# Two heads in the two row halves of the array: attention scores and maxima as pairs of 64-row tiles

## The chip, the cores and the metric

One core of a Trainium2 chip. The metric is the device time of one execution in microseconds (us); the time of a kernel is the median of its runs. Engines are named as in the profile: PE is TensorE's matmul part, PEld its weight loads, DVE VectorE, ACT ScalarE, POOL GpSimd, SP SyncE (here it only issues DMAs).

## The reference, cut to what matters

Two attention layers run one after the other on 8 batches of 256 rows of 320 channels, 20 heads of 16 channels each, with 256 context rows. The names in the kernel follow it: a *unit* `u` is one layer of one batch (0 to 7 are layer 0, 8 to 15 layer 1), `q` a running number of a pair of heads.

```python
# layer 0: 77 text tokens and 179 image tokens, one softmax each
q = split_heads(x @ Wq.T); k = split_heads(text @ Wk.T); v = split_heads(text @ Wv.T)
out_text = merge(softmax(q @ k.T / 4) @ v)
out_ip = merge(softmax(q @ k_ip.T / 4) @ v_ip)          # k_ip, v_ip from the image tokens
x = (out_text + out_ip) @ Wo.T + bo + x
# layer 1: 252 text tokens, 4 image tokens; the text weights also form
qsem = l2norm(probs_t @ text_ehs)                        # 512 wide, through a Gram matrix here
fused = q @ k_ip.T / 4 + 0.5 * (qsem @ l2norm(ip_ehs).T)
out = (probs_t @ v + (softmax(fused) * mask) @ v_ip) @ W_out + b_out + x
```

## The kernel before

Sixteen units follow one another, each in ten *slots* `j` (one pair of heads a slot), after a unit -1 that only prepares. `plan(u, j)` writes down by hand what a slot holds, and every engine walks the same plan, so each engine's order is fixed and an engine stops at the first wait that isn't met. In a slot of unit `u` the following stand in a row:

- `scores(q+1)`, line 505: two matmuls (one for each 128 of the 256 tokens `ch`) of 512 columns, two heads side by side, contracted over 100 rows: 96 of split queries and keys (`QP`, `KP`, tile rows 0 to 47 for head `a` = 0 and 48 to 95 for head 1, zero where the other head lies) and rows 96 to 99 that subtract each row's maximum.
- `weights(q+1)`, line 876 on ACT: the exponentials, from the two banks of the scores into `P`. In layer 1 `rounded_weights` (line 866) reads the same banks before that.
- `weigh(u, g)` in even slots, lines 537 to 551: four heads in four 32-column tiles of the array, from `P` (and in layer 1 `Y`) into `pPV`; ACT then copies `pPV` into `Vs` (`evacuate`, line 787) and only after that writes the exponentials of the slot.
- `quad(q, 0)` and `quad(q, 1)` in layer 1, line 519: four and three matmuls of 512 columns with the Gram matrix; DVE multiplies the result into `Y` (line 1116), POOL makes the `Y` it needs (line 1352).
- `maximum(u+1, h)`, line 482: for one head of the *next* unit two matmuls of 256 columns over 96 rows, into one bank; DVE reduces it (lines 1098, 1099 in layer 0, 1101 and 1103 in layer 1). The first of a slot stands before `weigh` in layer 0 and between the two `quad` in layer 1, the others among the projections. There are three in slots 0 to 5 and two in slot 6.
- pieces of the projections of unit `u+2` (lines 388, 415), then `values_back` (`nt`, line 560), and parts of the closing of unit `u-1` (`ot`, `op`, `soft` and others). `soft` in slot 1 of layer 1 makes DVE write `t` (line 1159) and ACT `ex` (line 896), ahead of the slot 2 work of both.

PE's results go to seven PSUM banks, `pB0` to `pB6`. `take` gives the bank that was given back longest ago and makes PE wait until what stood in it has been read (`freed`); so the order of the plan also sets which engine PE waits for.

In slot 7 `shift_rows(u+1)` turns the maxima (line 493); ACT writes `mhi`, DVE `mlo`, and `rows_out` (line 780) sends them by DMA into rows 96 to 99 of `QP`: in layer 0 two DMAs from ACT's queue and two from SP's, in layer 1 two from SP's. `scores` of the next unit, in slot 9, waits for them (`rows_landed`). In slot 8 SP issues the keys of unit `u+2` (line 764, `KP<-k0d`) behind those rows; the first `maximum` of the next unit's slot 0 waits for them (`pack_landed`). For units 8 and 9 POOL fills rows 96 to 99 with 1e20 first (line 1413).

Of the kernel before, what the change touches and what calls it, by code (L numbers as in the profile page):

```python
# [14 lines left out]
U = 2 * B  # L15
# [7 lines left out]
KROWS = 96  # L23
QROWS = 100
# [15 lines left out]
MAXH = (3, 3, 3, 3, 3, 3, 2, 0, 0, 0)  # L40
MAXF = (3, 3, 3, 3, 2, 2, 2, 2, 0, 0)
# [40 lines left out]
def plan(u, j):  # L82
# [17 lines left out]
    many = MAXF if u < 0 else MAXH  # L100
    heads = [("max", u + 1, h) for h in range(sum(many[:j]), sum(many[:j + 1]))] if u + 1 < U else []
    first, rest = heads[:1], heads[1:]
# [3 lines left out]
    scores = [("scores", q + 1)] if u >= 0 and q + 1 < U * NP else []  # L106
    weigh = [("weigh", *divmod(q // 2 - 1, NG))] if q >= 2 and q % 2 == 0 else []
    weigh += [("weights", q + 1)] if scores else []
    if u >= B:
        out += scores + weigh + [("quad", q, 0)] + first + [("quad", q, 1)]  # L110
    elif (u, j) in LATE_MAX:
        out += scores + weigh
        rest = heads
    else:
        out += scores + first + weigh
    out += pieces[0] + pieces[1] + rest[:1] + pieces[2] + rest[1:]
# [58 lines left out]
def build(nc, xT, cT, cipT, fs, Wq0, Wk0, Wv0, Wki0, Wvi0, Wo0, bo0,  # L175
          Wq1, Wk1, Wv1, Wki1, Wvi1, Wo1, bo1, ident_d, ind_d, hm_d, outT):
    with ExitStack() as ctx:
# [18 lines left out]
        wk = sb("wk", [128, 2, EC, C], F32R)  # L196
        wv = sb("wv", [128, 2, EC, C], F32R)
# [4 lines left out]
        ind = sb("ind", [4, 2, S], F32R)  # L202
# [12 lines left out]
        P = sb("P", [128, PR, 2, 2 * S])  # L215
        Y = sb("Y", [128, PR, 2, 2 * S])
# [5 lines left out]
        G = [flat(wk)[:, 0:896], flat(wk)[:, 896:1792], flat(wv)[:, 0:896]]  # L222
        PH = [[flat(wv)[:, 896 + 512 * i:896 + 512 * i + 512] for i in range(2)], [flat(w)[:, at:at + 512] for w, at in ((wv, 1920), (wk, 1792))]]
# [25 lines left out]
        Y_flat = Y[:, :, :, :].rearrange("p a b c -> p (a b c)")  # L249
# [66 lines left out]
        def ind_ready(u):  # L316
            u = u if u < 2 else B + u % 2 if u >= B else u % 2
            return l_ind[u], 16
# [14 lines left out]
        def tensor_program(_):  # L333
# [343 lines left out]
            for u in range(-1, U):  # L677
# [30 lines left out]
                if u < 0:  # L708
                    scores(0)
# [940 lines left out]
```

## Time and profile before

| | |
|---|---|
| median of 3 runs | 806.78 us (806.47 to 809.67) |
| profiled execution | 808.78 us, its span 806.8 us |
| PE / PEld busy | 762.5 / 616.4 us |
| DVE / ACT / POOL busy | 567.9 / 425.4 / 403.0 us |
| a unit of layer 0, of layer 1 | 37.8 us, 54.8 us |

A busy matmul counts from its start to its modelled end, and matmuls overlap in the array, so starts are read rather than durations: how far one row of the timeline starts after the row ahead of it, over the number of instructions in that. A wait shows in brackets at the row that waited.

### The profile page before, as it was taken

The page shows a single profiled execution, that of the slowest core. Times are in us where ns is not written, and L with a number is a line of the kernel's source. Part 1 is how long each engine was busy: PE and PEld are TensorE (multiplying, and loading weights), DVE is VectorE, ACT ScalarE, POOL GpSimd, SP SyncE. Part 2 cuts the span into 40 slices and gives each one's busy share as a digit, 9 for nine tenths or more (in the row PEclk, how much of TensorE's full clock was granted, in tenths as well). Part 3 has the DMA queues.
Part 4 walks back from the last instruction along what each step waited for, and adds up shares of the span by engine and source line. Part 5 has one row for each costly group of instructions (what it writes and reads, how often), then busy time and mean ns, then how long its engine had stood idle before and what let it go on. Part 6 is the DMA issues. An engine that isn't in the chain of part 4 may idle for free.

```text
span 806.8 us, 17013 instructions
## 1 busy us (share of the span) xinstructions
PE 762.5 (95%) x6246; PEld 616.4 (76%) x6246; DVE 567.9 (70%) x1575; ACT 425.4 (53%) x915; POOL 403.0 (50%) x297
## 2 busy tenths in 40 slices
PE   5889999999999999999999999999999999988896
PEld 5777788888788877777877778788777787766574
DVE  5357465757576676858768778698697797686745
ACT  5234646464637373646475565555655655555551
POOL 6511222020202040405568887787779778779763
PEclk9999999999999999999999999999999999999999
DMA  9854735654537372735252354153162332400010
GB/s 282 257 165 145 190 111 154 201 169 138 164 113 200 113 202 75 205 94 158 94 146 91 96 144 152 46 157 115 49 190 70 103 118 66 126 1 17 20 34 17
DMA packets 102514, 100.65 MB, mean 125 GB/s; under 512 B 9752, under 2 KB 101664, under 8 KB 102432
## 3 DMA queue, kind: packets, MB, share of 16 engines
q1 hardware_dynamic: 101952, 99.24, 42.2%
q8 instruction: 50, 0.82, 0.4%
q10 hardware_dynamic: 480, 0.33, 0.2%
q14 instruction: 32, 0.26, 0.1%
HBM read 61.65 MB, written 36.74 MB: 122 GB/s over the span
## 4 chain that ended last, share of the span: by engine, by line
PE 71%; DVE 9%; issue 5%; DMA 5%; ACT 4%; POOL 3%; SPq 2%; POOLq 0%; DVEq 0%; ACTq 0%
PE pB L388 19%; PE pB L519 12%; PE pB L482 8%; PE pB L505 7%; PE pB L603 5%; PE pPV L546 4%; PE pPV L541 4%; PE pPV L551 3%; DMA KP<-k0d 3%; PE pPV L537 2%; PE pB L560 2%; POOL Y L1352 2%; DVE m_sb L1101 2%; PE pB L415 1%; ACT P L876 1%
## 5 line engine op out<-in xcount | busy, mean ns | idle before, releaser
L1352 POOL TENSOR_TENSOR Y<-P,wv 128x512 f32<-128x512 f32 x120 | 157.0, 1326 | 106.6 <-ACT P L876 106.5
L1116 DVE TENSOR_TENSOR Y<-pB,Y 128x512 f32<-128x512 f32 x160 | 109.0, 686 | 67.3 <-PE pB L519 56.8
L482 PE MATMUL pB<-KP,QP 96*128 96x256 f32 x640 | 129.1, 287 | 5.0 <-DMA KP<-k0d 3.6
L1329 POOL TENSOR_TENSOR klo<-xin,khi 128x256 fp32r<-128x256 f32 x18 | 13.2, 756 | 232.1 <-ACT khi L787 232.1
L482 PEld LDWEIGHTS pB<-KP,QP 96*128 96x128 f32 x640 | 106.7, 191 | 17.8 <-issue 5.4
L1101 DVE TENSOR_REDUCE m_sb<-pB 128x2 f32<-128x504 f32 x160 | 108.0, 676 | 6.5 <-PE pB L482 5.3
L505 PE MATMUL pB<-QP,KP 100*128 100x512 f32 x320 | 109.8, 422 | 1.9 <-DMA QP<-mlo 1.5
L876 ACT ACTIVATE P<-pB 128x512 f32<-128x512 f32 x160 | 86.5, 597 | 39.5 <-PE pB L505 29.7
L866 ACT ACTIVATE wv<-pB 128x512 fp32r<-128x512 f32 x120 | 66.8, 591 | 67.3 <-PE pB L505 66.0
L876 ACT ACTIVATE P<-pB,ln 128x512 f32<-128x512 f32 x160 | 101.1, 691 | 0.0
L787 ACT ACTIVATE Vs<-pPV 128x512 f32<-128x512 f32 (+1 forms) x80 | 39.3, 492 | 104.7 <-PE pPV L541 71.3
L1099 DVE TENSOR_REDUCE m_sb<-pB 128x2 f32<-128x358 f32 x160 | 83.2, 520 | 0.0
L388 PE MATMUL pB<-cc,wki 128*128 128x256 f32 (+3 forms) x576 | 80.8, 273 | 0.1
L1098 DVE TENSOR_REDUCE m_sb<-pB 128x2 f32<-128x154 f32 x160 | 49.8, 312 | 41.7 <-PE pB L482 41.0
L519 PE MATMUL pB<-wv,wk 128*128 128x512 f32 x250 | 76.7, 410 | 2.5 <-DVE ipS L1103 2.4
L388 PEld LDWEIGHTS pB<-cc,wki 128*128 128x128 f32 (+1 forms) x576 | 70.6, 172 | 6.5 <-issue 4.1
L388 PE MATMUL pB<-wvi,cc 128*128 128x320 f32 (+1 forms) x384 | 68.0, 314 | 1.0 <-POOL wvi L1342 1.0
L388 PE MATMUL pB<-khi,wq 128*128 128x256 f32 (+1 forms) x288 | 56.7, 292 | 9.9 <-DVE wq L1001 8.5
L388 PEld LDWEIGHTS pB<-wvi,cc 128*128 128x128 f32 x384 | 60.0, 190 | 7.1 <-issue 4.5
L1375 POOL TENSOR_TENSOR rn<-n,mhalf 128x8 f32<-128x8 f32 (+2 forms) x17 | 57.1, 3358 | 15.6 <-DVE n L1147 15.6
L519 PEld LDWEIGHTS pB<-wv,wk 128*128 128x128 f32 x250 | 44.3, 189 | 21.1 <-issue 10.3
L505 PEld LDWEIGHTS pB<-QP,KP 100*128 100x128 f32 x320 | 50.8, 191 | 6.3 <-DMA QP<-mlo 2.3
(175 smaller groups left out, 1477.3 us busy)
## 6 DMA issues: line engine op xcount, KB each, us to landing
QP<-q0d SPq DMA_DIRECT2D x64, 192.0 KB, 4.1
KP<-k0d SPq DMA_DIRECT2D x64, 192.0 KB, 4.2
c_sb<-in_cT SPq DMA_DIRECT2D x16, 512.0 KB, 5.3
q0d<-qhi SPq DMA_DIRECT2D x32, 256.0 KB, 2.4
k0d<-khi SPq DMA_DIRECT2D x32, 256.0 KB, 2.4
q0d<-qlo SPq DMA_DIRECT2D x16, 256.0 KB, 2.5
k0d<-klo SPq DMA_DIRECT2D x16, 256.0 KB, 2.5
VB<-vipd SPq DMA_DIRECT2D x6, 640.0 KB, 3.8
```

Of the source, the lines that this page charges most:

```text
L388: made = mm(out, l, r, start=(n == 0), stop=(n == len(pairs) - 1))
L482: made = mm(bank[:, sc * S:sc * S + S], QP[i][0:KROWS, j, a, sc * 128:sc * 128 + 128], KP[i][0:KROWS, j, :], start=True, stop=True)
L505: mm(bank[:, :], KP[i][0:QROWS, j, ch * 128:ch * 128 + 128], QP[i][0:QROWS, j, :, :].rearrange("p a s -> p (a s)"), start=True, stop=True) ...
L519: made = mm(bank[:, :], G[i][:, col:col + 128], ph[src], start=(n == 0), stop=(n == len(jobs) - 1))
L866: act(PH[q % HR][ch], bank_of["sc", q, ch][:, :], ACT.Exp, scale=0.25).then_inc(ac_ph, 1)
L876: act(P[:, q % PR, ch, :], bank_of["sc", q, ch][:, :], ACT.Exp, scale=0.25, **twice).then_inc(ac_exp, 1)
L1098: nc.vector.tensor_reduce(m_sb[:, :, h], v[:, :, 0:TXT0], AX, ALU.max)
L1099: nc.vector.tensor_reduce(m_sb[:, :, H + h], v[:, :, TXT0:S], AX, ALU.max).then_inc(dv_mx, 1)
L1101: nc.vector.tensor_reduce(m_sb[:, :, h], v[:, :, 0:TXT1], AX, ALU.max)
L1116: tt(Y[:, p, dst, :], bank_of["gp", q, dst][:, :], Y[:, p, dst, :], MUL).then_inc(dv_y, 1)
L1352: tt(Y[:, p, ch, :], P[:, p, ch, :], PH[q % HR][ch].bitcast(F32), SUB).then_inc(po_y, 1)
L1375: tt(rn[:, :, hs], n2[:, :, hs], mhalf[:, 0:2 * n].rearrange("p (c h) -> p c h", c=2), POW).then_inc(po_rn, 1)
```

## The change

Each head gets 64 rows of `QP` and `KP` of its own: head 0 lies in rows 0 to 51, head 1 in rows 64 to 115 (48 of queries and keys, up to 4 that subtract the maximum). `maximum` becomes `maxima(u, j)`: both heads of a pair, four matmuls of 256 columns alternating between the row halves, head 0 into one bank and head 1 into another. `scores` in slots that also hold maxima is done in the same way, four matmuls of 256 columns and 52 rows in place of two of 512 (`halves`); in the other slots it stays two of 512 columns over 116 rows. `PAIRS` sets 2, 1, 2, 0, 2, 1, 2 pairs in slots 0 to 6, and they stand in one block right behind `scores`, ahead of `weigh` and `quad`; in unit -1 and in slot 0 of units 0 and 1 they stand behind most of the projections instead. Each scores bank now holds one head, so ACT writes by head, POOL waits for both heads. `rows_out` sends each row in two DMAs (one for each half), the indicator rows of `KP` go in two as well, and POOL's memset of 1e20 becomes two DMAs on SP's queue for units 8 and 9.

```diff
-MAXH = (3, 3, 3, 3, 3, 3, 2, 0, 0, 0)
-MAXF = (3, 3, 3, 3, 2, 2, 2, 2, 0, 0)
+PAIRS = (2, 1, 2, 0, 2, 1, 2, 0, 0, 0)
+PAIRS_FIRST = (2, 1, 2, 1, 1, 1, 1, 1, 0, 0)
...
+    scores = [("scores", q + 1, halves)] if u >= 0 and q + 1 < U * NP else []
+    out += scores
+    if halves:
+        out += pairs
+    out += [("weigh", *divmod(q // 2 - 1, NG))] if q >= 2 and q % 2 == 0 else []
+    out += [("weights", q + 1, halves)] if scores else []
     if u >= B:
-        out += scores + weigh + [("quad", q, 0)] + first + [("quad", q, 1)]
...
+        out += [("quad", q, 0), ("quad", q, 1)]
+    out += pieces[0] + pieces[1]
+    if late:
+        out += pairs
+    out += pieces[2]
...
+            def maxima(u, j):
+                i = u % 2
+                banks = [take("mx", u * H + 2 * j + a) for a in range(2)]
...
                 for sc in range(2):
+                    for a, bank in enumerate(banks):
+                        rows = half(a, KROWS)
+                        made = mm(bank[:, sc * S:sc * S + S], QP[i][rows, j, a, sc * 128:sc * 128 + 128], KP[i][rows, j, :],
+                                  start=True, stop=True)
...
+                    if halves:
+                        for a, bank in enumerate(banks):
+                            rows = half(a, QROWS)
+                            made = mm(bank[:, ch * S:ch * S + S], KP[i][rows, j, ts], QP[i][rows, j, a, :], start=True, stop=True)
...
             for r, tile, h0 in rows:
...
-                dma(QP[i][r:r + 1, :, :, :].bitcast(F32), tile[h0:h0 + H, :].bitcast(F32)).then_inc(l_m[i], 16)
+                for a in range(2):
+                    row = 64 * a + KROWS + r
+                    dma(QP[i][row:row + 1, :, a, :].bitcast(F32), tile[h0 + a:h0 + H:2, :].bitcast(F32)).then_inc(l_m[i], 16)
...
-                        nc.gpsimd.memset(QP[(u + 1) % 2][KROWS:QROWS, :, :, :].bitcast(F32), 1e20).then_inc(po_big, 1)
...
+                    for a in range(2):
+                        row = 64 * a + KROWS + 2
+                        dma(QP[u % 2][row:row + 1, :, a, :].bitcast(F32),
+                            ind[4:5, 1, None, :].to_broadcast([1, NP, S]).bitcast(F32)).then_inc(l_m[u % 2], 16)
```

Three places show what moves. The names: `KP0,QP0` are the next unit's (a maximum), `QP1,KP1` this unit's (scores), `wv` or `wkv` is a `quad`, `pPV` a `weigh`, `l_ld00` the landing of queries and keys, `ac_exp` the exponentials. First PE in slot 0 of unit 11, before:

```order
L505 MATMUL pB5<-QP1,KP1 128x512 [waits dv_op]
L505 MATMUL pB3<-QP1,KP1 128x512 [waits ac_exp]
L546 MATMUL pPV<-P,VY1 32x256 x8
L551 MATMUL pPV<-Y,y21 32x256 [waits dv_y]
L551 MATMUL pPV<-Y,y21 32x256 x7
L519 MATMUL pB6<-wv 128x512 [waits ac_ph,ac_exp]
L519 MATMUL pB6<-wv 128x512 x3
L482 MATMUL pB2<-KP0,QP0 128x256 [waits l_ld00]
```

and after:

```order
L492 MATMUL pB6<-KP0,QP0 128x256 [waits l_ld00,dv_y,ac_exp]
L492 MATMUL pB2<-KP0,QP0 128x256
L492 MATMUL pB6<-KP0,QP0 128x256
L492 MATMUL pB2<-KP0,QP0 128x256
L492 MATMUL pB3<-KP0,QP0 128x256 [waits dv_op,dv_y]
L492 MATMUL pB4<-KP0,QP0 128x256
L492 MATMUL pB3<-KP0,QP0 128x256
L492 MATMUL pB4<-KP0,QP0 128x256
L569 MATMUL pPV<-P,VY1 32x256 x8
L574 MATMUL pPV<-Y,y21 32x256 x8
```

The first matmul that needs the next unit's keys has moved ahead of `weigh` and of the first `quad`. Next PE in slot 2 of unit 11, from its scores on, before:

```order
L505 MATMUL pB0<-QP1,KP1 128x512 [waits dv_mx]
L505 MATMUL pB5<-QP1,KP1 128x512 [waits dv_y]
L546 MATMUL pPV<-P,VY2 32x256 x8
L551 MATMUL pPV<-Y,y21 32x256 x8
L519 MATMUL pB4<-wv 128x512 [waits ac_ph,dv_bg,ac_bg]
L519 MATMUL pB4<-wv 128x512 x3
```

and after (left out are the eight matmuls of the maxima, into `pB0`, `pB6`, `pB1` and `pB2`):

```order
L522 MATMUL pB4<-QP1,KP1 128x256 [waits dv_mx]
L522 MATMUL pB5<-QP1,KP1 128x256
L522 MATMUL pB4<-QP1,KP1 128x256
L522 MATMUL pB5<-QP1,KP1 128x256
...
L569 MATMUL pPV<-P,VY2 32x256 x8
L574 MATMUL pPV<-Y,y21 32x256 x8
L542 MATMUL pB4<-wkv 128x512 [waits ac_ph,ac_exp]
L542 MATMUL pB4<-wkv 128x512 x3
L542 MATMUL pB5<-wkv 128x512 [waits ac_exp]
L542 MATMUL pB5<-wkv 128x512 x2
```

The first `quad` now goes into `pB4`, the bank of this same slot's scores, where it had another bank. Last SP around slot 7 of unit 4, before:

```order
L735 DMA k1d6<-klo 64x256
L780 DMA QP1<-mlo 1x20x256 [waits dv_sr,ac_sr]
L780 DMA QP1<-mlo 1x20x256
L764 DMA KP0<-k0d6 48x4x256 [waits l_k]
L764 DMA KP0<-k0d6 48x4x256
```

and after:

```order
L758 DMA k1d6<-klo 64x256
L803 DMA QP1<-mlo 1x10x256 [waits dv_sr,ac_sr]
L803 DMA QP1<-mlo 1x10x256 x3
L787 DMA KP0<-k0d6 48x4x256 [waits l_k]
L787 DMA KP0<-k0d6 48x4x256
```

Four DMAs of the row `mlo` stand ahead of the keys where two stood.

## Rows read from the trace of the kernel before

**Rows 1.** The page: busy time of the engines; the chain that ended last.

```profile
PE 762.5 (95%) x6246; PEld 616.4 (76%) x6246; DVE 567.9 (70%) x1575; ACT 425.4 (53%) x915; POOL 403.0 (50%) x297
...
PE 71%; DVE 9%; issue 5%; DMA 5%; ACT 4%; POOL 3%; SPq 2%; POOLq 0%; DVEq 0%; ACTq 0%
```

**Rows 2.** Busy time by stretch: unit 5, unit 10 (columns in the first row).

```profile
core 0: us, PE busy (x) PEld busy (x) DVE busy (x) ACT busy (x) POOL busy (x), PEclk, DMA share, GB/s
246.40:284.20 37.80, 37.66 (x347) 31.71 (x344) 25.81 (x76) 20.91 (x47) 4.24 (x6) 1.00 0.58 165
472.30:527.10 54.80, 53.97 (x431) 43.19 (x429) 44.64 (x117) 31.14 (x66) 43.08 (x30) 1.00 0.38 114
```

**Rows 3.** Timeline of PE, unit 2: start us, us, engine, line, operation.

```profile
150.97 0.40 PE L482 MATMUL pB<-KP,QP 96*128 96x256 f32 x2
151.30 0.64 PE L537 MATMUL pPV<-P,VX 77*32 77x256 f32 x8
...
156.87 0.63 PE L505 MATMUL pB<-QP,KP 100*128 100x512 f32 x2
157.34 0.40 PE L482 MATMUL pB<-KP,QP 96*128 96x256 f32 x2
157.58 0.66 PE L388 MATMUL pB<-cc,wki 128*64 128x180 f32 x6
```

**Rows 4.** Weight loads by line and shape (busy us, mean ns | idle); timeline of eight loads.

```profile
L482 PEld LDWEIGHTS pB<-KP,QP 96*128 96x128 f32 x640 | 106.7, 191 | 17.8 <-issue 5.4 <-DVE m_sb L1099 1.5 <-ACT P L876 0.8
...
L537 PEld LDWEIGHTS pPV<-P,VX 77*32 77x32 f32 x320 | 6.3, 108 | 7.6 <-issue 3.6
...
151.30 0.16 PEld L537 LDWEIGHTS pPV<-P,VX 77*32 77x32 f32 x8
```

**Rows 5.** Timeline of slot 4 of unit 11: PE and ACT around a weighing.

```profile
553.25 1.07 PE L546 MATMUL pPV<-P,VY 128*32 128x256 f32 x16
...
554.13 1.05 PE L551 MATMUL pPV<-Y,y 128*32 128x256 f32 x16
...
555.11 1.20 PE L519 MATMUL pB<-wv 128*128 128x512 f32 x4
555.25 0.38 ACT L787 ACTIVATE Vs<-pPV 128x256 f32<-128x256 f32 x1 [1.04 <-PE pPV L551]
...
555.53 1.26 ACT L876 ACTIVATE P<-pB,ln 128x512 f32<-128x512 f32 x2
```

**Rows 6.** Timeline of slot 2 of unit 11: PE and ACT.

```profile
544.33 1.21 PE L519 MATMUL pB<-wv 128*128 128x512 f32 x4
...
544.88 0.34 ACT L896 ACTIVATE ex<-t 128x160 f32<-128x160 f32 x1 [2.76 <-DVE t L1159]
...
546.34 1.28 ACT L876 ACTIVATE P<-pB,ln 128x512 f32<-128x512 f32 x2
```

**Rows 7.** Timelines of SP's queue and PE from unit 4's slot 7 to unit 5's slot 0.

```profile
242.08 1.64 SPq L780 DMA_DIRECT2D QP<-mlo  x2
243.76 1.25 SPq L764 DMA_DIRECT2D KP<-k0d  x2
...
246.38 0.71 PE L505 MATMUL pB<-QP,KP 100*128 100x512 f32 x2
...
248.58 0.47 PE L482 MATMUL pB<-KP,QP 96*128 96x256 f32 x2
```

**Rows 8.** DMA issues by line: KB each, median us from issue to landing.

```profile
KP<-k0d SPq DMA_DIRECT2D x64, 192.0 KB, 4.2
...
KP<-k1d SPq DMA_DIRECT2D x32, 96.0 KB, 3.1
```

**Rows 9.** Timelines of SP's queue and PE from unit 11's slot 8 into slot 0.

```profile
529.08 1.27 SPq L764 DMA_DIRECT2D KP<-k0d  x2
...
531.03 0.63 PE L505 MATMUL pB<-QP,KP 100*128 100x512 f32 x2
...
533.46 1.19 PE L519 MATMUL pB<-wv 128*128 128x512 f32 x4
534.48 0.40 PE L482 MATMUL pB<-KP,QP 96*128 96x256 f32 x2
```

**Rows 10.** Waits: engine line waited for: us in total, times, longest.

```profile
PE pB L493 <- DVE ipS L1103: 4.3, 8, 1.7
```

More of the change, by code:

```diff
@@ L22 @@
 NP = H // 2
-KROWS = 96
-QROWS = 100
+KROWS = 48
+QROWS = 52
+IROWS = 16
 PR = 3
@@ L99, in plan @@
         pieces = [[], [], []]
-    many = MAXF if u < 0 else MAXH
-    heads = [("max", u + 1, h) for h in range(sum(many[:j]), sum(many[:j + 1]))] if u + 1 < U else []
-    first, rest = heads[:1], heads[1:]
+    many = PAIRS_FIRST if u < 0 else PAIRS
+    pairs = [("max", u + 1, jj) for jj in range(sum(many[:j]), sum(many[:j + 1]))] if u + 1 < U else []
+    late = u < 0 or (u, j) in LATE_MAX
+    halves = bool(pairs) and not late
     out = []
@@ L495, in shift_rows, with scores @@
                 give(bank)
-            def scores(q):
+            def scores(q, halves):
                 u, j = divmod(q, NP)
@@ L502, in scores @@
                 pe.wait_ge(*ind_ready(u))
+                banks = [take("sc", q, n) for n in range(2)]
                 for ch in range(2):
-                    bank = take("sc", q, ch)
-                    mm(bank[:, :], KP[i][0:QROWS, j, ch * 128:ch * 128 + 128],
-                       QP[i][0:QROWS, j, :, :].rearrange("p a s -> p (a s)"), start=True, stop=True).then_inc(pe_sc, 1)
+                    ts = slice(ch * 128, ch * 128 + 128)
+                    if halves:
+                        for a, bank in enumerate(banks):
+                            rows = half(a, QROWS)
+                            made = mm(bank[:, ch * S:ch * S + S], KP[i][rows, j, ts], QP[i][rows, j, a, :], start=True, stop=True)
+                            if ch == 1:
+                                made.then_inc(pe_sc, 1)
+                    else:
+                        rows = slice(0, 64 + QROWS)
+                        mm(banks[ch][:, :], KP[i][rows, j, ts], QP[i][rows, j, :, :].rearrange("p a s -> p (a s)"),
+                           start=True, stop=True).then_inc(pe_sc, 1)
+                for bank in banks:
                     give(bank)
@@ L681, in tensor_program @@
                         if what == "max":
-                            maximum(*a)
+                            maxima(*a)
                         elif what == "bg":
@@ L708, in tensor_program @@
                 if u < 0:
-                    scores(0)
+                    scores(0, False)
             weigh(U - 1, NG - 1)
@@ L1280, in vector_program @@
                         if what == "max":
-                            maximum(*a)
+                            for h in (2 * a[1], 2 * a[1] + 1):
+                                maximum(a[0], h)
                         elif what == "done":
```

144 lines of the change are left out of this document (69 added, 75 removed).

## The prediction

> **What bounds the kernel now.** The page first: PE is busy for 95% of the span and makes up 71% of the chain that ended last [rows 1]. By stretch it is the same everywhere, but its margin is not: in unit 5 (layer 0) PE is busy 37.7 of 37.8 us and DVE 25.8 (68%); in unit 10 (layer 1) PE 54.0 of 54.8, DVE 44.6 (81%) and POOL 43.1 (79%) [rows 2]. So time saved on PE is time saved until one of four late arrivals takes over: a bank that ACT or DVE has not read yet, the rows of maxima, the next unit's keys, or DVE itself. The timelines show how far off each is, and it is very little. I read them at the places to which the change moves a wait.
>
> **What PE saves.** Starts in the timeline: two maximum matmuls take 157.34 to 157.58, 0.12 us each; two of the scores 156.87 to 157.34, 0.235 each [rows 3]. Two heads in two row halves should stream at once, two matmuls of 256 columns in the 0.12 us of one.
> - Maxima: a pair has four matmuls, 0.48 us before, 0.24 after; 160 pairs (10 in each of 16 preparing stretches): -38.4 us.
> - Scores: of 160 slots 88 are done by halves (slots 0, 1, 2, 4, 5, 6 of units 0 to 14, less slot 0 of units 0 and 1): 0.47 before, 0.24 after: -20.2 us.
> - Change of tiling: before the column tiles of a weighing the last maximum pair takes 150.97 to 151.30, 0.33 where 0.24 is usual [rows 3]; after it 554.13 to 555.11 is 0.98, where the sixteen ahead of it took 0.88 [rows 5]. So a change costs 0.09 to 0.10 us. Even slots with a block gain one (full, halves, columns, full), odd ones and the late blocks two: 58 + 60 + 20 = 138 changes: +13.8 us.
>
> Whether the pair really runs at once hangs on the weight loads, which the trace shows for columns only. A load of 128 columns takes 191 ns in the records, one of 32 columns 108 [rows 4]: 0.86 ns a column, so about 110 ns of loading for 128, as long as the 0.12 us of the matmul it hides behind. Side by side in both halves that still fits; one after the other it would take 0.22 us a pair of matmuls and eat the gain. Eight loads of 32 columns for the weighing all stand within 0.16 us, each of them 108 ns [rows 4], so they do overlap between column tiles. I take "at once"; the other is a rival. (The Trainium skill, TensorEngine Tiling (Array Packing), Key Properties, says that different tiles load and multiply in parallel and that a changed tiling mode drains the array; the drain agrees with the 0.09 us of the rows, the parallel load in row halves no row here shows.)
>
> PE alone would thus give -44.8 us. Now what comes late.
>
> **Rows of maxima (slot 7 to 9, layer 0).** Two `mlo` DMAs are issued in 1.64 us, 0.82 each, the last at 242.9; small loads into these tiles land 3.1 us after issue [rows 7, 8], so at 246.0, and the scores that wait for them start at 246.38 [rows 7]. Slots 7 to 9 hold no maxima, so PE gets there as before. The rows go out in four DMAs now: two more at 0.8 each, 1.6 us, less about 0.2 of slack (0.4 by the median): +1.5 for each of units 0 to 7, 12 us. At unit 8 four more stand on SP (two halves, two of 1e20): 3.2 less some slack, +2.7. The POOL memset that goes hid behind other work and gives nothing back. If half a row costs half the issue the term falls from 14.7 to 7.
>
> **Keys.** SP issues the keys right behind these rows in layer 0: the second at 244.4, which lands 4.2 later at 248.6 [rows 7, 8], and the first maximum starts at 248.58 [rows 7]. No slack: they come 1.6 later, PE has lost 1.5 of that already; and in unit 8: +2 in all. In layer 1 they are anchored to the closing of the unit before, not to the rows: issued at 529.1 and 529.7, landing at 533.9; the first maximum starts at 534.48 [rows 8, 9], late, because weighing and the first quad stand ahead of it. In the new order it stands 0.3 behind scores that start at 531.03 [rows 9]: 531.3. PE then waits 2.6 us, and weighing and both quads queue behind it.
>
> **Banks behind the exponentials.** In even slots 2, 4, 6 of layer 1 the first quad now takes a bank of this slot's scores. ACT frees it after `Vs`, which waits for the weighing, and one exponential: `Vs` starts at 555.25, the exponentials at 555.53, the first done at 556.2; the quad starts at 555.11 [rows 5]. So 1.1 us of idle PE where no other bank was needed before. Slots 4 and 6, units 8 to 13: 12 x 1.1 = +13.2. In layer 0 it is the last piece of the projections in slot 4 (seven short matmuls cover part of it) and `nt`: 0.5 a unit, and one late slot 0: +5.
>
> **Slots 0 to 2 of layer 1.** In slot 2 ACT is later still: `ex` waits for DVE's `t`, and only then come the roundings, `Vs` and the exponentials from 546.34, the first done at 547.0, against the quad's start at 544.33 [rows 6]: 2.7. That chain starts with DVE, which has as many maxima and products ahead of `t` as before, and starts its maxima about 1.9 later through the keys: exponential at 548.9. PE without waits would be at 543.8 (544.33, -0.9 for slots 0 and 1, -0.2 for the scores, +0.6 for two pairs and a change). 5.1 us, keys included. The seven units differ in how early their keys are (unit 8 and 9 have slack, 14 waited already): I take 4.2 as a mean, +29.3 us. It is the largest term, and the least sure: 2 to 5 a unit.
>
> **Given back.** The shift in slot 7 waited for the last maximum, 4.3 us over 8 units [rows 10]; the block in slot 6 stands earlier: -4.3.
>
> **Sum**: -38.4 - 20.2 + 13.8 + 14.7 + 2 + 13.2 + 5 + 29.3 - 4.3 = +15.1 us. Against the profiled execution's own 808.8 that is 823.9; the median of the runs is 2.0 lower, 806.8, so I forecast 822 (824 for an execution like the profiled one).
>
> (The Trainium skill, TensorEngine Tiling, PSUM Bottleneck, warns that tiling speeds TensorE but not the reading of PSUM. That is the mechanism of the terms on banks, in this kernel's order; without it the sum would be some 40 us lower.)
>
> **Rivals.**
> 1. *Loads of the two halves go one after the other.* Then a pair of matmuls takes two loads, 0.22 us, and pair and scores gain next to nothing: -4.8 and -1.8 in place of -58.6. Some 12 us of that are hidden in slots 0 to 2 of layer 1, which wait anyway: 822 + 52 - 12 = 862. Against it: the overlapping column loads; for it: no row shows a load in a row half. 0.18.
> 2. *The chain to the exponentials is not late, and half rows cost half.* DVE then keeps up in slots 0 and 1 (it has 19% of the unit idle, and the odd slots lose a maximum), so slots 0 to 2 cost 1.2 each unit, 8 rather than 29, and the rows 7 rather than 15: 822 - 21 - 8 = 793, faster than before. It decides from a mean cost of some 2 us in slots 0 to 2. Against it: keys and `t` are both read as late, by rows. 0.11.
> 3. *Nothing but PE counts*, all waits hidden: 762. 0.03.
> 4. *The forecast*, with its terms off by up to their bounds: 808 to 845. 0.62, of which 0.03 lies within 4 us of before.
> 5. Between 1 and 4, a load that overlaps in part: 845 to 860. 0.06.
>
> **How the numbers follow.** 822, the likeliest. The range leaves out rival 3, a third of rival 2 and most of rival 1: 792 to 852. 0.5% is about what a measurement of this kernel can tell from no change, 802.7 to 810.8. Faster: rivals 3 and 2, 0.13. Same: 0.07, from the edges of 2 and 4. Slower: 0.80.
>
> **What would show it.** Right: maxima in blocks of four starting at 0.12 a pair; PE waits before L542 for the exponentials of about 1.1 us in slots 4 and 6 of units 8 to 13, and more in slot 2; a wait for keys at L492 in slot 0 of layer 1, of 2 to 3 us; a wait for `QP<-mlo` before the scores of slot 9 in each unit of layer 0; units of layer 0 near 37 us and of layer 1 near 58. Wrong: a cadence of 0.22 a pair (rival 1); layer 1 units under 54.8 (rival 2); no wait on `mlo` (the rows' price). If units of layer 0 are slower than 38, the price of pairs or of changes of tiling is off.

## The result, and the profile after

| | before | after |
|---|---|---|
| median of 4 runs, us | 808.22 (806.47 to 809.96) | 870.74 (865.26 to 876.89) |
| profiled execution, us (span) | 808.78 (806.8) | 865.26 (863.5) |
| granted clock, mean of the span | 0.989 | 0.974 (0.959 to 0.964 in the other runs) |

The change makes the kernel 7.7% slower: ratio 1.0771, 95% interval 1.0728 to 1.0814. I had forecast 822 us, range 792 to 852. The sign was right, the size was not: +62.5 us where +15 was worked out.

The page of after has this row where the first of [rows 1] stood. PE's busy time fell by only 8 us, while the span grew by 57:

```profile
PE 754.8 (87%) x6422; PEld 581.0 (67%) x6422; DVE 573.1 (66%) x1575; ACT 424.3 (49%) x915; POOL 394.5 (46%) x295
```

The same two units as in [rows 2], unit 5 and unit 10, with the same columns. Both are longer, and in both PE is busy for less time than before (36.4 for 37.7, 52.7 for 54.0), DVE, ACT and POOL for as long as before:

```profile
249.90:289.50 39.60, 36.37 (x359) 29.08 (x357) 25.76 (x76) 20.62 (x47) 4.23 (x6) 1.00 0.58 157
493.20:553.30 60.10, 52.71 (x442) 40.83 (x441) 45.45 (x117) 31.17 (x66) 43.23 (x30) 1.00 0.36 103
```

**What stops PE now.** Waits of PE in after (line waited for: us in total, times, longest). L492 are the maxima, L542 the quads, L583 the transposes of values:

```profile
PE pB L542 <- ACT P L905: 24.7, 19, 2.5
PE pB L492 <- DMA KP<-k0d: 20.9, 12, 2.8
PE pB L492 <- DVE klo L1030: 9.0, 9, 1.2
...
PE pB L492 <- DVE alo L1030: 7.7, 8, 1.7
PE pB L583 <- ACT Vs L810: 6.1, 9, 2.8
...
PE pB L492 <- DVE qlo L1030: 3.1, 7, 0.7
```

In before the quads never waited for an exponential, the maxima never for a low part, and for keys they waited 3.6 us:

```profile
PE pB L482 <- DMA KP<-k0d: 3.6, 4, 2.5
```

**The balance.** I walked PE's instructions from start to start. The time up to the next start is PE's own, less what the records show as idle; of the time at 1.2 GHz, the lower of the clock's two levels, half counts as lost to the clock. The 8.5 us ahead of PE's first instruction are left out. Over the profiled executions, in us:

| | before | after | difference |
|---|---|---|---|
| PE's own work, at the full clock | 757.0 | 735.5 | -21.5 |
| idle ahead of an instruction | 32.8 | 97.3 | +64.5 |
| lost to the clock (half of 17.1 and 44.4 us at 1.2 GHz) | 8.6 | 22.2 | +13.6 |

That is +56.6, the whole difference between the two profiled executions. The other runs of after had a lower clock still, and the median is some 5 us longer than the profiled one. Three things are to be explained: a gain of 21.5 where I had 44.8, waits of 64.5 where I had 60, but partly in other places, and the clock, for which I had nothing.

**The pairs do run at once.** Timeline of PE, unit 4 of after: one block of two pairs between scores by halves and a weighing.

```profile
229.64 0.50 PE L522 MATMUL pB<-QP,KP 52*128 52x256 f32 x4
229.98 0.64 PE L492 MATMUL pB<-KP,QP 48*128 48x256 f32 x8
230.55 0.64 PE L560 MATMUL pPV<-P,VX 77*32 77x256 f32 x8
```

Eight maximum matmuls take 0.57 us to the next start; one after the other they would take 0.95. In the records the two heads' matmuls here start 4 ns apart and the next two 0.118 us later, so the weight loads of the halves overlap and rival 1 falls. But the four matmuls of the scores take 0.34 us and not 0.24: the first load in a new tiling stands exposed, 0.10 us, and it has no place in my sum.

**The first long wait.** Unit 12, slot 0: the scores at 620.84, then PE stands still until the keys have landed. I had worked out 2.6 us from the rows of unit 11. In units 10 to 14 it is 1.9 to 2.8 (2.81 in unit 11), here 2.14.

```profile
620.84 0.50 PE L522 MATMUL pB<-QP,KP 52*128 52x256 f32 x4
623.48 0.74 PE L492 MATMUL pB<-KP,QP 48*128 48x256 f32 x8 [2.14 <-DMA KP<-k0d]
624.15 1.51 PE L569 MATMUL pPV<-P,VY 128*32 128x256 f32 x16
```

What follows shows in the windows of the same place: for 3.42 us right behind this wait PE has a granted clock of 0.50, that is 1.2 of 2.4 GHz, and the sixteen matmuls of L569, usually 0.88, take 1.26 to the next start.

```profile
616.80:624.63 7.83, 5.69 (x48) 4.47 (x50) 7.38 (x17) 4.82 (x11) 7.83 (x3) 1.00 0.68 147
624.63:628.05 3.42, 3.42 (x30) 1.68 (x23) 2.47 (x8) 0.64 (x2) 0.95 (x1) 0.50 1.11 223
```

**The exponentials.** Unit 11, slot 2, the place of [rows 6]:

```profile
574.48 0.50 PE L492 MATMUL pB<-KP,QP 48*128 48x256 f32 x4 [0.34 <-DVE qlo L1030]
574.91 1.07 PE L569 MATMUL pPV<-P,VY 128*32 128x256 f32 x16
...
576.18 0.34 ACT L925 ACTIVATE ex<-t 128x160 f32<-128x160 f32 x1 [2.41 <-DVE t L1189]
...
577.38 0.39 ACT L810 ACTIVATE Vs<-pPV 128x256 f32<-128x256 f32 x1
...
577.64 1.28 ACT L905 ACTIVATE P<-pB,ln 128x512 f32<-128x512 f32 x2
...
578.40 1.89 PE L542 MATMUL pB<-wkv 128*128 128x512 f32 x7 [1.55 <-ACT P L905]
```

The chain is the one I described: `ex` waits for DVE's `t`, and only behind it come the roundings, `Vs` and the exponential that frees the quad's bank.

### The profile page after: what moved, and what is told of

The parts are those of the page before. It is cut to its first block and busy times, and to the rows that moved or that the text cites. A ratio compares the mean times of both kernels' runs of the same rounds, so it can differ in the third digit from the quotient of the medians.

```text
span 863.5 us, 17573 instructions
## 1 busy us (share of the span) xinstructions
PE 754.8 (87%) x6422; PEld 581.0 (67%) x6422; DVE 573.1 (66%) x1575; ACT 424.3 (49%) x915; POOL 394.5 (46%) x295
## 5 line engine op out<-in xcount | busy, mean ns | idle before, releaser
L1384 POOL TENSOR_TENSOR Y<-P,wkv 128x512 f32<-128x512 f32 x160 | 207.6, 1321 | 158.6 <-ACT P L905 158.1
L542 PE MATMUL pB<-wkv 128*128 128x512 f32 x560 | 152.4, 409 | 25.8 <-ACT P L905 24.7
L542 PEld LDWEIGHTS pB<-wkv 128*128 128x128 f32 x560 | 101.1, 190 | 71.6 <-ACT P L905 36.1
L895 ACT ACTIVATE wkv<-pB 128x512 fp32r<-128x512 f32 x160 | 86.3, 592 | 75.2 <-PE pB L522 36.7
L492 PE MATMUL pB<-KP,QP 48*128 48x256 f32 x640 | 67.1, 299 | 45.6 <-DMA KP<-k0d 20.9
L492 PEld LDWEIGHTS pB<-KP,QP 48*128 48x128 f32 x640 | 48.9, 187 | 56.6 <-issue 45.1
L395 PE MATMUL pB<-cc,wki 128*128 128x256 f32 (+3 forms) x576 | 76.1, 276 | 1.5 <-ACT P L905 1.5
L395 PEld LDWEIGHTS pB<-cc,wki 128*128 128x128 f32 (+1 forms) x576 | 68.3, 172 | 11.4 <-issue 4.5
L395 PEld LDWEIGHTS pB<-khi,wq 128*128 128x128 f32 (+1 forms) x288 | 42.9, 182 | 15.9 <-DVE wq L1030 8.5
L527 PE MATMUL pB<-QP,KP 116*128 116x512 f32 x144 | 50.4, 433 | 2.6 <-DMA QP<-ind 1.6
```

Source lines behind the costliest of these rows:

```text
L395: made = mm(out, l, r, start=(n == 0), stop=(n == len(pairs) - 1))
L492: made = mm(bank[:, sc * S:sc * S + S], QP[i][rows, j, a, sc * 128:sc * 128 + 128], KP[i][rows, j, :], start=True, stop=True)
L527: mm(banks[ch][:, :], KP[i][rows, j, ts], QP[i][rows, j, :, :].rearrange("p a s -> p (a s)"), start=True, stop=True).then_inc(pe_sc, 1)
L542: made = mm(bank[:, :], G[i][:, col:col + 128], ph[:, src, :, :].rearrange("p a s -> p (a s)"), start=(n == 0), stop=(n == len(jobs) - 1))
L895: act(split(PH[q % HR], n, halves), scored(q, n), ACT.Exp, scale=0.25).then_inc(ac_ph, 1)
L1384: tt(y, w, r.bitcast(F32), SUB).then_inc(po_y, 1)
```

## The experiments

Theory A: the place of the blocks is the loss (keys, exponentials and low parts are late there). Theory B: the halves themselves cost (changes of tiling, exposed loads). Theory C: the clock is a loss of its own. Each run is given with the kernel before timed beside it.

### Slot 0 behind the projections

```
-LATE_MAX = ((0, 0), (1, 0))
+LATE_MAX = tuple((u, 0) for u in range(U))
```

> The changed kernel, but in slot 0 of every unit the pairs stand behind the projections (and the scores of that slot go over full rows), as they do in units 0 and 1. Theory A (the place of the blocks costs: keys and banks are late there): the wait for keys before the first maximum (20.9 us in all, nearly all in slot 0) goes, what is left of it is 3 us or less; the scores of 13 slots cost 0.23 more each (+3); part of what slot 0 gives comes back as a later wait in slot 2, since DVE gets the maxima no sooner. 850 to 860 us against 870.7. Theory B (the row halves themselves cost: changes of tiling, exposed weight loads): the time stays within 4 us of 870. Theory C (the clock: waits let it fall and that costs most): as A, and the time at 1.2 GHz (44 us) falls by a third.

854.7 us, ratio 1.0564 (1.0512 to 1.0617), against 1.0771: 16 us less. The wait for keys is gone from the waits of PE; units 2 to 4 of layer 0 take 38.7, 38.6 and 38.7 us where they took 41.3, 38.7 and 38.9. Theory A as written, B's "within 4 us" is out. Theory C is not borne out as written: the time at 1.2 GHz should have fallen by a third and fell from 44 to 41 us. In the units whose wait had gone, 10 to 13, there was none, but units 5 and 9 have stretches where after has none.

### Every block behind the projections

```
+LATE_MAX = tuple((u, j) for u in range(U) for j in range(NP))
```

> The changed kernel with every block of pairs behind the projection pieces of its slot; maxima stay pairs in the two row halves, all scores go over full rows. Theory A: the waits before maxima and before the quads (71 us of the 97 that PE waits) go back to about 10, the time at 1.2 GHz from 44 to about 20; PE's own work is 745 without the clock, + 20 for full scores, - 5 for fewer changes of tiling: 760, with 45 of waits and 8 for the clock 813 us, range 800 to 825: about as before (808). Theory B: the pairs still cost their changes and exposed loads, and the time stays above 840. Rival within A: DVE then gets the maxima of a slot in one late heap and the shift in slot 7 waits for it; units of layer 1 then stay near 58 us.

856.8 us (1.0586; 1.0522 to 1.0649). 813 was wrong. The quads waited 0, as expected, but the shift took the wait over, as in the rival inside A:

```profile
PE pB L505 <- DVE ipS L1132: 17.1, 8, 3.9
PE pB L505 <- DVE m_sb L1128: 12.2, 8, 2.3
```

Maxima at the end of a slot reach DVE in a heap, and in slot 7 the shift stands behind the last of them. Own work was also 2 us a unit above the changed kernel's in layer 0 (38.2 for 36.3): full scores and isolated blocks. The time at 1.2 GHz, expected to fall to about 20 us, was 47.8.

### The order alone

```
-                        rows = half(a, KROWS)
+                        rows = slice(0, 64 + KROWS)
...
-    scores = [("scores", q + 1, halves)] if u >= 0 and q + 1 < U * NP else []
+    scores = [("scores", q + 1, False)] if u >= 0 and q + 1 < U * NP else []
```

> The order of the changed kernel without the halves: maxima and scores of every slot over full rows (112 and 116), one after the other, the blocks where the change puts them. The maxima then take in rows that hold the mask, so the result is not the reference's; every operation of the other engines is the same. Theory A: PE does 58 us more of work, less 19 for changes of tiling and first loads, and much of that is hidden under the same waits: 865 to 885 us, no quicker than the changed kernel, with waits of 50 to 70 us. Theory B: without row halves the time falls below 850.

910.4 us (1.1266; 1.1189 to 1.1343), above the range. The edit brought a wait of its own: the full rows need the rows of `ind`, which I had overlooked.

```profile
PE pB L493 <- DMA KP<-ind: 35.2, 4, 10.3
PE pB L543 <- ACT P L906: 23.2, 20, 2.3
PE pB L493 <- DMA KP<-k0d: 16.7, 9, 2.9
```

So the total says little; the units without that wait do: own work 38.3 us in units 3 to 5 and 54.4 in units 10 to 13, where the changed kernel has 36.3 and 52.4. The halves save 2.0 us a unit against the same order over full rows, 32 us in sixteen units; my 58.6 less 13.8 for changes is 44.8. The waits for exponentials and keys are there without any half: they belong to the order. And this order costs 0.7 and 0.3 us a unit of own work against before, with no half in it. (Its matmuls also go over 112 and 116 rows where before has 96 and 100; no run separates the two.)

### Full scores

```
-    scores = [("scores", q + 1, halves)] if u >= 0 and q + 1 < U * NP else []
+    scores = [("scores", q + 1, False)] if u >= 0 and q + 1 < U * NP else []
```

> The changed kernel with all scores over full rows, blocks of maxima still in halves and still ahead of the weighing. Plain sum: 88 slots by 0.23 us are 20 us more of PE work with the same number of changes of tiling, half of it under waits: 875 to 885. Rival D (scores by halves make the exponentials late: both banks are done only at the end, where over full rows the first is done 0.23 us sooner, and GpSimd waits for both): the time is at or below 870, and the waits of quads for the exponentials (24.7 us) fall by a third or more.

868.6 us (1.0732; 1.0674 to 1.0791), level with the changed kernel. Own work rises by 1.0 us a unit and the waits fall by as much (7.7 to 6.8 in units 10 to 13). The scores by halves, 20 us of my sum, give nothing in this order. The quads' wait did not fall by a third (23.9 for 24.7), so rival D's reason is not shown; the plain sum is wrong as well.

### Blocks of two in the odd slots

```
-PAIRS = (2, 1, 2, 0, 2, 1, 2, 0, 0, 0)
+PAIRS = (1, 2, 1, 2, 1, 2, 1, 0, 0, 0)
```

> The changed kernel with the blocks of two pairs in the odd slots (1, 2, 1, 2, 1, 2, 1 pairs in slots 0 to 6), where no weighing follows. Theory A1 (the quads wait for the exponentials because a block of two pairs, the scores and the weighing come together in an even slot): the 24.7 us of the quads' wait for ACT fall under 8, the wait for keys stays; 840 to 852 us. Theory A2 (the DVE is what is late and hands banks back late wherever the block stands): the waits move to the odd slots, their sum falls by less than 10 us, 858 to 868.

848.2 us (1.0486; 1.0416 to 1.0555). The time is inside A1's range, with a little more left than it said:

```profile
PE pB L492 <- DMA KP<-k0d: 20.4, 12, 2.6
PE pB L542 <- ACT P L905: 9.6, 12, 0.9
```

The wait for keys is there as in the changed kernel (20.4 for 20.9), the quads' fell from 24.7 to 9.6. The waits are those of the profiled execution, which took 858.2 us, 10 more than the median.

### The second pair behind the projections

```
-    if halves:
-        out += pairs
+    if halves:
+        out += pairs[:1]
...
-    if late:
-        out += pairs
+    out += pairs if late else pairs[1:]
```

> The changed kernel, but of a block of two pairs only the first stands ahead of the weighing and the second behind the projection pieces. Theory A1: no slot takes more than six banks before its quads: their wait for the exponentials falls under 5 us; keys stay (20 us); 10 to 12 more changes of tiling than now in each unit (+ 0.5 us each unit); 840 to 850. Theory A2: 858 or more.

838.6 us (1.0338; 1.0294 to 1.0381), the best single move: 32 us, 1.4 more than A1 allowed. The quads' wait is gone, the wait for low parts ahead of maxima fell from 19.8 to 0.9, and the keys' stays (17.9). Some of it came back at the shift (13.3 us, DVE) and before late pairs (7.5, ACT). A1 holds: a slot with two pairs ahead takes 2 + 4 banks, the projection under way holds the last of the seven, and so the first quad gets one that ACT still has to read. With one pair ahead it does not.

### The pairs alone

In layer 0 the first pair of a slot behind the scores, in layer 1 between the quads, a second one behind the projections, 2, 1, 2, 1, 2, 1, 1 pairs, full scores:

```
+    first = [] if late else pairs[:1]
+    if u < B:
+        out += first
...
-        out += [("quad", q, 0), ("quad", q, 1)]
+        out += [("quad", q, 0)] + first + [("quad", q, 1)]
```

> The order of the kernel before as near as pairs allow (2, 1, 2, 1, 2, 1, 1 pairs; the first of a slot behind the scores in layer 0 and between the quads in layer 1, a second one behind the projection pieces), with maxima as pairs in halves and all scores over full rows. PE's own work: 10 pairs save 2.4 us in a unit, 20 changes of tiling (0.09) and 10 exposed first loads (0.10) cost 2.8: as before, 54 in layer 1 and 37.6 in layer 0. Theory A: waits are nearly those of before, 808 to 822 us. Rival (heads that come two at a time are late for DVE and for the banks whatever the order): waits of 2 us and more in each unit, 830 to 850.

825.0 us (1.0175; 1.0138 to 1.0211), 3 us above the range. The window of unit 10: PE is never idle, and yet the unit is no shorter than before (54.9; before 54.8 with 0.8 idle):

```profile
485.90:540.80 54.90, 54.90 (x430) 40.87 (x429) 44.12 (x117) 31.10 (x66) 43.03 (x30) 1.00 0.39 113
```

So ten pairs, which save 2.4 us of matmuls, raise the own work by 0.9 (54.9 for 54.05): their changes and loads cost 3.3 us, 0.33 a block. This is theory B's part. With so few waits there is no time at 1.2 GHz in units 0 to 14 either.

### Half of DVE's maxima

```
-                    nc.vector.tensor_reduce(m_sb[:, :, h], v[:, :, 0:TXT1], AX, ALU.max)
+                    nc.vector.tensor_reduce(m_sb[:, :, h], v[:, :, 0:TXT1 // 2], AX, ALU.max)
```

(and 88 of 179 columns in layer 0)

> The changed kernel with half of DVE's work on the maxima taken away: the maxima of the scores of 88 of 179 and 126 of 252 columns only, so the result is not the reference's; PE, ACT and GpSimd do the same. DVE is busy some 2.5 us less in a unit of layer 0 and 5 in one of layer 1. Theory A2 (DVE is late): the waits for low parts (20 us) and for the exponentials (24.7) fall by half or more, 835 to 850 us. Theory A1 (the place and ACT's own order make them late): they stay, 862 to 870.

864.7 us (1.0676; 1.0629 to 1.0723). The waits did not move:

```profile
PE pB L542 <- ACT P L905: 25.6, 20, 2.8
PE pB L492 <- DMA KP<-k0d: 21.0, 13, 2.8
PE pB L492 <- DVE klo L1030: 9.0, 9, 1.2
...
PE pB L492 <- DVE alo L1030: 8.0, 8, 1.7
```

DVE's load is not the cause, though its name stands in two of the rows. Slot 4 of unit 11 in the trace of after shows what is:

```profile
585.49 0.57 ACT L810 ACTIVATE khi<-pB 128x504 fp32r<-128x504 f32 x1
585.61 0.31 PEld L492 LDWEIGHTS pB<-KP,QP 48*128 48x128 f32 x4
585.72 0.40 PE L492 MATMUL pB<-KP,QP 48*128 48x256 f32 x4
...
586.09 0.47 DVE L1030 TENSOR_TENSOR klo<-kip,khi 128x8 fp32r<-128x8 f32 x1 [1.02 <-ACT khi L810]
586.49 0.67 DVE L1030 TENSOR_TENSOR klo<-pB,khi 128x504 fp32r<-128x504 f32 x1
...
587.30 0.50 PE L492 MATMUL pB<-KP,QP 48*128 48x256 f32 x4 [1.19 <-DVE klo L1030]
```

The second pair of the block wants the bank of the projection that has just ended. DVE, idle for 1.02 us, waits for ACT's copy of it and reads the bank only then.

### Both moves together

Slot 0 behind the projections and second pairs late.

> The changed kernel with both moves that took waits away, together: slot 0 of every unit behind the projections, and in the other slots only the first pair of a block ahead of the weighing. Theory A (waits and the clock that they take along are the loss; own work of PE is then 37.4 us in units 3 to 5 and 53.2 in 10 to 13 where the kernel before has 37.6 and 54.05): the waits fall to some 1 us a unit and the time at 1.2 GHz in units 8 to 14 to 7 us or less; 812 to 824 us, at best level with before, since the pairs have almost nothing to give. Rival (the pairs still have 20 us in them): 800 or less. Rival (the two moves take the same wait): 835.

825.9 us (1.0194; 1.0162 to 1.0227): 45 us less than the changed kernel, where the two moves alone took 16 and 32. They are nearly additive, so they take different waits. The waits did not fall to 1 us a unit but to 1.9 in units 10 to 13, 1.1 of it before maxima and 0.7 at the shift, and the time is 2 us above the range. Units 8 to 14 still have 13.6 us at 1.2 GHz where I had said 7 or less.

### Half rows in the kernel before

```
-                dma(QP[i][r:r + 1, :, :, :].bitcast(F32), tile[h0:h0 + H, :].bitcast(F32)).then_inc(l_m[i], 16)
+                for a in range(2):
+                    dma(QP[i][r:r + 1, :, a, :].bitcast(F32), tile[h0 + a:h0 + H:2, :].bitcast(F32)).then_inc(l_m[i], 16)
```

> The kernel before with one part of the change alone: each row of maxima goes out as two DMAs of half the heads, 8 in place of 4 in each unit of layer 0, 4 in place of 2 in layer 1. The prediction's term: 1.5 us a unit in layer 0, 12 and more in all: 819 to 824 us. Rival (a half row is issued in the same 0.8 us but lands sooner, as the trace of the changed kernel has it: 2.05 us after the last issue): 0.5 us a unit, 810 to 814.

818.1 us against 809.8, ratio 1.0099 (1.0074 to 1.0125): 8 us, 6 to 10. That is between my 14.7 and the rival, but it is not the wait that I had priced. PE waits for `mlo` once, in unit 0, for 1.1 us (1.5 in before), and in no other unit of layer 0. Two other waits grew, from 3.6 us for keys and 4.7 for the transposes' `Vs`:

```profile
PE pB L560 <- ACT Vs L788: 7.1, 10, 2.8
PE pB L482 <- DMA KP<-k0d: 6.9, 7, 3.2
```

Between the two profiled executions the clock took 3.4 us more, too. The later `Vs` has a cause at hand that I had overlooked: ACT's own queue also sends two rows in layer 0, four now, ahead of its exponentials and the next `Vs`. Around slot 7 of unit 4, before and with half rows:

```profile
241.26 1.52 ACTq L780 DMA_DIRECT2D QP<-mhi  x2
```

```profile
246.62 3.05 ACTq L781 DMA_DIRECT2D QP<-mhi  x4
```

No run halves ACT's rows alone, so this stays argued. On SP's side the trace of after shows why the scores of slot 9 need not wait. SP's queue and PE from unit 4 to unit 5, the place of [rows 7]:

```profile
245.28 3.15 SPq L803 DMA_DIRECT2D QP<-mlo  x4
248.47 0.61 SPq L787 DMA_DIRECT2D KP<-k0d  x1
```

```profile
249.52 0.63 PE L583 MATMUL pB<-ident,Vs 128*128 128x128 f32 x4 [0.23 <-ACT Vs L810]
249.91 0.71 PE L527 MATMUL pB<-QP,KP 116*128 116x512 f32 x2
```

Four issues take 3.15 us, 0.79 each, as expected. But by the semaphore's records the last half row lands 2.05 to 2.07 us after its issue begins (six places in layer 0), where the last whole row in before took 3.1 to 3.5. I had taken 3.1 for both. Half rows so delay the rows by some 0.5 us and not by 1.6, and 0.2 of that is behind PE's wait for `Vs`.

### The wait for keys filled

Seven matmuls of 512 columns in units 8 to 14, into the bank that the maxima then overwrite:

```
+                for _ in range(7 if j == 0 and u > B else 0):
+                    mm(banks[0][:, :], wo[:, 0, 0, 0:128], wo[:, 0, 1:3, 0:256], start=True, stop=True)
                 pe.wait_ge(*pack_landed(u, j // 4))
```

> The changed kernel with seven matmuls of 512 columns (1.65 us, results overwritten) put ahead of the wait for keys in slot 0 of units 8 to 14, where PE stands idle for 1.8 us and more. Theory C (the idle time takes the clock down and that is a loss of its own): PE reaches the first maximum when it did, and the stretches at 1.2 GHz that begin some 7 us into units 10 to 14 (3.4 us each, at least five) do not come: 8 to 12 us less than the changed kernel, 858 to 864. Rival (the row halves and small tiles take the clock down, not the idle time): the stretches stay, and the time is that of the changed kernel or some us more.

859.6 us (1.0598; 1.0559 to 1.0637) against 1.0771: 11 us less, with 12 us more of matmuls. The granted clock of its four runs is 0.974 to 0.986, that of after's 0.959 to 0.974. (The two profiled executions, after's fastest and this kernel's slowest, are only 4 us apart; there the clock's share is 6.8 us.) The same slot of unit 12:

```profile
621.26 0.50 PE L524 MATMUL pB<-QP,KP 52*128 52x256 f32 x4
621.69 1.88 PE L488 MATMUL pB<-wo 128*128 128x512 f32 x7
623.95 0.74 PE L494 MATMUL pB<-KP,QP 48*128 48x256 f32 x8 [0.39 <-DMA KP<-k0d]
624.62 1.07 PE L571 MATMUL pPV<-P,VY 128*32 128x256 f32 x16
```

The maxima come 2.69 us behind the scores, as in after (2.64), and the clock stays, in this stretch and in the whole of unit 12:

```profile
625.00:628.40 3.40, 3.40 (x39) 1.99 (x28) 3.19 (x9) 1.54 (x3) 1.16 (x2) 1.00 1.12 217
...
617.20:677.70 60.50, 54.65 (x450) 42.15 (x449) 45.52 (x117) 31.12 (x66) 43.28 (x30) 1.00 0.38 103
```

Theory C is shown for this wait: with the same halves and small tiles in place, the stretches of units 11 to 13 went with the idle time ahead of them, so it was the idle time that took the clock down. It does not do so each time. Of units 8 to 13 only unit 9 has such a stretch left, behind a quad's wait of 2.44 us, and in after the same wait was 2.52 us and no stretch followed. Two others came in units 3 and 5, where nothing was edited and after has none. In units 2 to 14 of after nine waits are 1.9 us or longer, and at six of them the clock fell.

### Pairs alone, halves for the scores of layer 0

```
-    halves = bool(pairs) and not late
+    halves = bool(pairs) and not late and u < B
```

on the kernel of the pairs alone, with the scores by that flag.

> The order of the kernel before with pairs (as in the run of the pairs alone, 825 us), and in layer 0, where the first pair of a slot stands right behind the scores, the scores of these slots by halves too: seven slots of a unit save 0.23 us each and no change of tiling is added, 1.6 us a unit, 12 in all. Theory A (a saving on PE counts where no wait takes it up): PE's own work in units 3 to 5 falls from 38.2 to 36.8 us and the time to 813 to 818 us. Rival (in layer 0 what follows is late already: keys and rows in slots 9 and 0, banks of the exponentials; the run by halves or by full rows showed no difference in the changed kernel): own work falls, the waits rise from 1.7 by as much, and the time stays at 822 to 827.

821.0 us (1.0158; 1.0131 to 1.0185), between the two. Own work fell by 1.5 us a unit as the theory says, the waits did not rise (1.7 to 1.3), but the time fell by 4 us (825.0 to 821.0) and not by 7 to 12, and by the ratios (1.0175 and 1.0158) the difference is within the noise. In the trace units 3 to 5 are 1.3 to 2.5 us shorter and unit 2 is longer by 1.2, with 3.4 us at 1.2 GHz in it.

### One early pair a slot

```
-LATE_MAX = ((0, 0), (1, 0))
-PAIRS = (2, 1, 2, 0, 2, 1, 2, 0, 0, 0)
+LATE_MAX = tuple((u, 0) for u in range(U))
+PAIRS = (2, 1, 2, 1, 2, 1, 1, 0, 0, 0)
```

with the first pair ahead of the weighing and the second late.

> All that took waits away, in one kernel: slot 0 behind the projections, 2, 1, 2, 1, 2, 1, 1 pairs, the first of a slot ahead of the weighing with its scores by halves (so that the change of tiling to the columns is shared), a second one behind the projections. Own work of PE by the rows so far: 37.2 us in units 3 to 5, 53.5 in 10 to 13; waits 1.3 and 1.2. Theory A: 812 to 822, best of the versions with pairs, still not under before, because the half rows (8 us) and the changes of tiling have eaten what the pairs save. Rival (something is left in the pairs): 804 or less.

818.1 us, ratio 1.0098 (1.0062 to 1.0135), the best with pairs. Take off the half rows' 8 us and it stands where before stands; that is an estimate, no run does it. The pairs are not worth nothing here: by the balance of its profiled execution PE's own work is 743.8 us, 13 less than in before, changes of tiling included. But PE is idle for 47.2 us where before has 32.8, and the time at 1.2 GHz is 41.0 us for 17.1, which costs 12. Nothing I found beats the kernel before.

### The price of a block

One matmul of 256 columns ahead of the maximum of each even head in the kernel before, over 48 rows (half tiling) and over 96 (no change of tiling):

```
+                if a == 0:
+                    mm(bank[:, 0:S], QP[i][0:KROWS // 2, j, 0, 0:128], KP[i][0:KROWS // 2, j, :], start=True, stop=True)
```

> The kernel before with one matmul of 48 rows and 256 columns ahead of the maximum of every even head (160 in all), its result overwritten: a matmul of the half tiling put between full ones, so two changes of tiling and one exposed load, 160 times. The prediction's price (0.09 to 0.10 for a change, no exposed load): with 0.12 us of its own, 0.31 each, 50 us in all at most. Theory of the rows (an isolated block costs about 0.3 us beside its matmuls): 0.42 each, 67 us at most. A part is hidden under waits in both.

> The same with the added matmul over 96 rows: no change of tiling, the same 256 columns. 0.12 us each, 19 us in all, on both theories; the difference to the run with 48 rows is the price of an isolated block: 160 by 0.19 = 30 us by the prediction, 160 by 0.3 = 48 us by the rows.

873.9 us (1.0786; 1.0755 to 1.0817) and 821.7 (1.0140; 1.0108 to 1.0172): 52 us apart, over 160 blocks 0.33 us each (0.30 to 0.36), not the 0.19 of the prediction. The timelines show where it sits. Over 48 rows the next start is 0.31 us away, over 96 rows 0.12:

```profile
205.59 0.38 PE L482 MATMUL pB<-KP,QP 48*128 48x256 f32 x1
205.90 0.50 PE L484 MATMUL pB<-KP,QP 96*128 96x256 f32 x2
```

```profile
203.46 0.28 PE L482 MATMUL pB<-KP,QP 96*128 96x256 f32 x1
203.58 0.41 PE L484 MATMUL pB<-KP,QP 96*128 96x256 f32 x2
```

That is 0.19 on the way out. On the way in, the last matmul of 256 columns ahead of the added one takes 0.21 to the next start where 0.12 is usual (31 such places), 0.09. The remaining 0.05 of the 0.33 I can't place.

## Why the prediction was wrong, point by point

- **Which waits.** Right in kind: PE was left idle in slot 0 by keys, in slots 2, 4 and 6 of layer 1 by exponentials. The sizes of layer 1 held: in units 8 to 13 the wait for the exponentials was 1.08 us in slots 4 and 6 each (I had 1.1), and over units 9 to 13 keys, exponentials and `qlo` in slots 0 to 2 came to 3.9 us a unit (I had 4.2). The shift's wait fell from 7.3 to 1.7 us (I had -4.3, from one of its two rows). That the waits come to 64.5 us for my 60 is luck all the same: low parts, 20 us without a term, stand against 14 that the rows of maxima did not cost as a wait and some 5 too many for keys and exponentials in slots 0 to 2 of layer 1.
- **What PE saves.** This is the first term that failed: -21.5 us for -44.8. The matmuls of a pair cost 0.118 us as worked out. The change of tiling was mis-sized: I took it from the one change that the trace of before shows, into and out of column tiles with loads of 32 columns [rows 3, 5], and so had no exposed load. An isolated block costs 0.33 us, not 0.2 (measured with one small matmul in the block; ten lone pairs a unit gave the same). In a unit of the changed kernel two blocks stand isolated (slots 1 and 5) and four share a change with the weighing. At the measured price these six cost some 0.7 us a unit more than my 0.1 a change, about 11 us in all, and the new order itself takes 0.3 to 0.7 us of own work a unit (order alone), about 8. The 4 us left I can't place.
- **Low parts.** The second: no term for them. The block asks for four banks at once and gets some whose low part DVE has not read: `klo`, `alo`, `qlo`, 19.8 us. I had followed ACT as the reader of banks and not DVE, which reads the same ones behind ACT. With one pair ahead they were 0.9 us.
- **Keys of layer 0.** I had +2 over the rows' delay; the wait in slot 0 is 2.0 us in unit 2 and 1.0 to 1.2 in units 3 to 6, 6.3 in all for 0.7 in before. With half rows alone it was 3.1. The keys come later behind the rows, and the block now also stands 0.3 us behind the scores, which I had worked out for layer 1 and not for layer 0.
- **The clock.** The third: no term. Waits of about 2 us, of which I had predicted several, are often followed by 3.4 us and more at 1.2 GHz: 13.6 us lost in the profiled execution, more in the others. That a filled wait gives back 11 us shows it.
- **Rows of maxima.** The wrong wait, and too high. In after PE waits for `mlo` 0.9 us in all, in unit 0, and 1.6 in unit 8 for the rows of 1e20 (before: 1.5 in unit 0), where I had 1.5 in each unit and 14.7 in all. A half row lands 1.1 us sooner than I took it to. Half rows do cost 8 us, but through keys, `Vs` and the clock.
- **Put together**, for the profiled execution, by the balance: 823.9 + 23.3 (own work) + 4.6 (waits) + 13.6 (clock) = 865.4, against 865.3. The median is 5 us above it, with a lower clock.
- **The signs** that I had named: cadence, quads' waits of 1.1 us and the wait for keys came as written (the keys in units 10 to 14; 1.2 us in unit 8, none in unit 9). The wait for `mlo` in each unit of layer 0 did not. Units 2 to 7 took 38.7 us and more, not near 37, and that was my sign for a wrong price of pairs or of changes of tiling, which it was in part; units 8 to 13 took 58.9 to 63.5, not near 58.
- **Rivals.** Rival 1, with 862 the nearest number to 870.7, was wrong as a mechanism: loads of the halves overlap. It named the right place, the weight load, but it is the first load of a tiling, not every one. Rivals 2 and 3 are out; of rival 2 the 7 us for the rows was near the measured 8, but for another reason than it gave: a half row still takes 0.79 us to issue. The range, up to 852, left out the case of three unpriced costs of one sign.

What stays open: why the order alone costs own work on PE, where the 4 us of own work and 0.05 us of a block are, and what part of the half rows' 8 us is clock (the profiled execution with half rows had 3.4 us more at 1.2 GHz in its start and 3.4 in its end).

## What to carry to other kernels

Price a packed tile by its block, not by its matmul: entry, first load and exit were 0.33 us here, more than one pair of 256 columns saves (0.24), so only blocks that share their edges with a change that is there anyway can pay. When work is gathered into a block, list every reader of every bank that it takes, at its new place, and not only the engine that seems next. And add to a wait of two microseconds on this engine the half clock that may follow it: here it did at six of nine, and each such stretch of 3.4 us costs 1.7.

## What the runs showed of the hardware

- Matmuls in the two row halves start 4 ns apart, and with new weights each time a pair of them takes 0.118 us: the loads are hidden in both halves (the rows of unit 4 above). The Trainium skill, TensorEngine Tiling (Array Packing), Key Properties, says that different tiles load and multiply in parallel; the trace agrees. It also says that a changed tiling mode drains the array. What a change takes here is 0.09 us going in and 0.19 coming out in the runs with a matmul between.
- The same page, Restrictions and Gotchas, says that row tiling raises the pressure on PSUM, since different row tiles write to different banks. Here it is 4 banks of 7 for a block of two pairs; with one pair in its place the quads' wait of 24.7 us was gone.
- I had not expected waits of 2 us to cost clock. Each of the eight stretches at 1.2 GHz that after has in units 2 to 14 follows close on waits of 1.2 to 2.7 us in all; in unit 12 it was one wait of 2.14 us, and with it filled the stretch did not come. Not each such wait is followed by one: waits of 2.52 us (unit 9) and 1.94 (unit 10) were not.
- A DMA of one row costs its queue about as much for half the heads: 0.79 us for 10 KB, 0.82 for 20. The half row lands sooner, 2.05 us after its issue begins for 3.1 and more.
